# Value products of a half group: one block in every fourth unit instead of a piece in each

## What is computed

```python
q = _rms_norm(q, g_q)
k = _rms_norm(k, g_k)
logits = jnp.einsum('bhqd,bhkd->bhqk', q, k) * d ** (-0.5)
attn = jax.nn.softmax(logits, axis=-1)
o = jnp.einsum('bhqk,bhkd->bhqd', attn, v)
o = jnp.swapaxes(o, 1, 2).reshape(b, n, dim)
return o + o @ W_out
```

## Time and profile before

| | us |
|---|---|
| median of 3 runs | 2251.61 (2249.65 to 2253.29) |
| the profiled execution's own time | 2247.79 |
| its span | 2246.0 |
| attention loops, from the turn of unit 4 to the end of the tail, four batches together | 241.03 |
| PE busy, whole span | 2129.1 (95%) |
| VectorE busy | 1630.1 (73%) |
| ScalarE busy | 1293.8 (58%) |
| POOL busy | 527.2 (23%) |
| value products (L2023), mean duration of a pass in the first loop | 0.391 |
| turns (L2005), same | 0.274 |
| scores (L1989), same | 0.384 |

### The profile page before, as it was taken

The page is one execution under the profiler, slowest core; times in us unless marked ns, Lnnn a source line. Parts: engine busy times, 40 slices in busy tenths (PEclk is TensorE's granted clock), DMA queues, the critical chain, the costliest instruction groups (busy, mean ns, idle before and its releaser), DMA issues.

```text
span 2246.0 us, 135671 instructions
## 1 busy us (share of the span) xinstructions
PE 2129.1 (95%) x57232; PEld 1830.8 (82%) x57232; DVE 1630.1 (73%) x6269; ACT 1293.8 (58%) x5763; POOL 527.2 (23%) x2255
## 2 busy tenths in 40 slices
PE   5768999999989999999999999999999999999998
PEld 3654555645545899999999999999999999999997
DVE  7987967878678487777677776667766666766665
ACT  6765947758568345555556655555555545555553
POOL 2002121021120222332233322222222222222221
PEclk8559999999999999999999999999999999999999
DMA  5000000010010000000000000000000000000000
GB/s 208 3 2 1 1 1 1 1 57 1 1 57 1 22 5 5 5 1 1 1 1 1 1 11 1 1 11 1 1 11 1 1 1 10 1 1 11 13 9 14
DMA packets 8410, 26.49 MB, mean 12 GB/s; under 512 B 1028, under 2 KB 1352, under 8 KB 7880
## 3 DMA queue, kind: packets, MB, share of 16 engines
q1 hardware_dynamic: 7712, 23.07, 2.8%
q10 hardware_dynamic: 424, 0.07, 0.0%
HBM read 18.94 MB, written 4.19 MB: 10 GB/s over the span
## 4 chain that ended last, share of the span: by engine, by line
PE 80%; DVE 12%; ACT 4%; issue 2%; DMA 1%; POOL 0%; SPq 0%; DVEq 0%; POOLq 0%; ACTq 0%
PE psum L2257 54%; PE psum L2218 8%; PE psum L2005 3%; PE psum L1926 3%; PE psum L1968 2%; PE psum L2023 2%; PE psum L2103 2%; PE psum L1989 2%; DVE region_cols L1232 2%; DVE region_cols L1248 2%; DVE top L1425 2%; ACT region_rows L786 1%; PE psum L1945 1%; DMA region_cols<-in_L_cond_W_emb_dram 1%; PE psum L1902 1%
## 5 line engine op out<-in xcount | busy, mean ns | idle before, releaser
L2257 PE MATMUL psum<-partsA,region_w_hh 128*128 128x40 f16 x24576 | 855.3, 179 | 10.4 <-issue 4.8
L2257 PE MATMUL psum<-partsB,region_w_hh 128*128 128x40 f16 x24576 | 853.3, 179 | 0.6 <-issue 0.5
L2257 PEld LDWEIGHTS psum<-partsA,region_w_hh 128*128 128x128 f16 x24576 | 758.7, 96 | 37.1 <-issue 11.2
L2257 PEld LDWEIGHTS psum<-partsB,region_w_hh 128*128 128x128 f16 x24576 | 724.1, 96 | 1.1 <-issue 0.5
L599 POOL TENSOR_TENSOR region_w_b<-region_w_b 128x16 f32<-128x16 f32 x1022 | 245.3, 240 | 1078.4 <-DVE region_w_b L1751 1078.4
L1725 DVE TENSOR_REDUCE psum<-psum 128x8 f32<-128x32 f32 x1024 | 201.7, 197 | 198.6 <-PE psum L2257 187.7
L1061 ACT ACTIVATE mixA<-psum 128x8 f32<-128x8 f32 x512 | 95.3, 186 | 428.3 <-DVE psum L1725 428.3
L1075 ACT ACTIVATE region_w_b<-psum 128x8 f32<-128x8 f32 x1024 | 190.0, 186 | 144.0 <-DVE psum L1740 86.9
L601 POOL COPY region_work<-region_w_b 128x8 f32<-128x8 f32 x1024 | 230.9, 225 | 2.2 <-DVE region_w_b L1751 2.2
L1751 DVE TENSOR_TENSOR_SCAN region_w_b<-giveB,region_w_b 128x40 f32<-128x40 f32 x512 | 123.8, 242 | 129.0 <-ACT region_w_b L1075 129.0
L1732 DVE TENSOR_REDUCE psum<-psum 128x8 f32<-128x32 f32 x1024 | 191.1, 187 | 0.7 <-PE psum L2257 0.6
(11 more groups left out here) (265 smaller groups left out, 2820.9 us busy)
## 6 DMA issues: line engine op xcount, KB each, us to landing
region_rows<-in_x_dram SPq DMA_DIRECT2D x4, 1024.0 KB, 11.1
region_w_a<-in_L_cond_W_qkv_dram SPq DMA_DIRECT2D x1, 3072.0 KB, 23.4
region_w_hh<-in_L_cond_W_hh_dram SPq DMA_DIRECT2D x4, 768.0 KB, 6.3
region_w_a<-in_L_cond_W_ih_dram SPq DMA_DIRECT2D x1, 3072.0 KB, 9.9
out_dram<-region_w_b SPq DMA_DIRECT2D x12, 256.0 KB, 2.2
region_cols<-in_L_cond_W_emb_dram SPq DMA_DIRECT2D x1, 2048.0 KB, 19.5
region_cond<-in_cond_dram SPq DMA_DIRECT2D x1, 1024.0 KB, 11.0
region_w_a<-in_L_cond_W_out_dram SPq DMA_DIRECT2D x1, 1024.0 KB, 21.5
```

The costliest lines, as they stand in the source:

```text
L2257: made = e.matmul(k.slots(bank)[:, :, ch, :, 0:2], k.w16[:, 2 * read + c, part, NC * "rzn".index(g) + 2 * half + ch], k.parts[read][:, c]. ...
```

## The change

```diff
+VALUES_TURNS = {2: 0}
...
         if n + AHEAD < len(UNITS):
             pe_scores(e, k, b, n + AHEAD)
         pe_turn(e, k, b, n)
-        if n >= 4:
-            group, kt = divmod(n - 4, 4)
-            pe_weighted_values(e, k, b, group // 2, group % 2, kt)
+        if n >= 4 and n % 4 in VALUES_TURNS:
+            group, first = n // 4 - 1, VALUES_TURNS[n % 4]
+            for kt in range(first, first + NT // len(VALUES_TURNS)):
+                pe_weighted_values(e, k, b, group // 2, group % 2, kt)
             if group % 2 == 1 and kt == NT - 1:
                 pe_divide(e, k, b, group // 2)
```

## The result

| | before | after |
|---|---|---|
| median, us | 2251.41 (2249.65 to 2253.29, 4 runs) | 2285.44 (2284.99 to 2287.71, 4 runs) |
| profiled execution, its span | 2247.79, 2246.0 | 2287.71, 2286.0 |
| ratio, 95% interval | | 1.0152 (1.0137 to 1.0167) |

The changed kernel is 34.0 us slower by the medians. The forecast was 2287 against a median of 2251.6, 35.6 us more.

The account below looks back on a forecast made before the run. PE was taken as the bound at 1.98 us a unit, only 0.15 ahead of ScalarE. Half groups of 9.08 and 10.32 plus ends made 69.13 a batch, 35.6 more over four: 2287 us, range 2270 to 2300.

Parts of the forecast that it names:

- The ready work at the block's start: At the block's start in the attention loop, VectorE has only its copy left, 0.68; ScalarE one copy and exponentials, 0.60 + 1.34.
- PE's total decides: Rival for the attention loops: the block is absorbed, a half group costs 7.51, time 2240; chance 6%.
- The block's price: A block of 16 value products on PE takes 1.87 us; upper end 2.28 if standing together gains nothing.
- The two sums: Block start to next block start in the loop: 9.08 us for an undivided half group, 10.32 with a divide.
- The ends: Loop ends: turn 4 to the first block 5.25 us; seventh block (unit 30) to the tail block 3.81.
- The total: Turn 4 to the tail's end takes 69.13 us a batch, 8.90 more than before; four batches make 35.6.
- no change: Rival for the attention loops: stall and saving meet, a half group stays at 7.92, time near 2252; chance 4%.
- A short stall: Rival: the block's unit costs 3.28, the next three 1.83 each; half group 8.77, time 2275; chance 15%.
- The clock rival: PE's pauses in each unit lower the granted clock; at 0.65 the loops cost 115 us more, 2367; chance 3%.
- granted clock 1.00: Sign expected in the profile after: the granted clock stays at 1.00.
- no wait of value products for the divide copy: Sign in the loops: ScalarE's divide copy lies two units ahead of its reader, so that wait goes.
- one chain that starts with them: Chain after each block: scores, maxima, copy, reciprocal, maxima, neg_top, exponentials, copy, turn, next block; 9.08 us undivided.

Follow-up runs that it names:

- the half maxima with pieces: The kernel before with VectorE's row maxima over 256 of the 512 keys, value products still a piece in each unit: 2236.74 us, ratio 0.9947.
- the unit at 262.90 above: A regular unit of the kernel before reordered to turn, next scores, then the piece of value products, from unit 4 on: 2247.07 us, ratio 0.9991.

## Why the prediction was right

**What bounds the kernel.** Right: PE's full row of 1.98 a unit is a bound of its own, as the half maxima with pieces showed, and the others stand little behind it: in the undivided half group after the change turns that ScalarE's copy releases are still 1.83 apart (263.87 to 265.70).

**The ready work at the block's start.** The prediction gave VectorE only its copy, 0.68, because its maxima of unit m+2 "began before the turn". Its own rows say otherwise: the turn starts at 238.58 and the maxima at 238.78, and they run past the value products' start at 239.55. After the change the maxima of 256.95 and the copy of 258.09 keep VectorE at work until 258.77, 1.03 behind the block's start. The sum does not use the 0.68. The rejection of "PE's total decides" does, and it holds with 1.03 too, since that is still under the 2.31 which that case needs.

**The block's price.** 1.87 was taken, with 2.28 as the other end. Every block in the trace of after lasts 1.93 in the timeline and 1.87 to the next start, as the tail in the earlier trace rows, apart from two on a lowered clock. The prediction's estimate of 1.47 rested on the speedup that the Trainium skill, TensorE: Matmul & The Clock Gate, Part 3, "Measured speedup vs the span model", states for three column tiles. The four column tiles of these fp32 products took 1.87, and the measurement decides.

**The two sums.** Undivided 9.08 against 8.96, divided 10.32 against 10.29. The difference of the first lies in two links: the reciprocal to the next maxima (0.24 taken, 0.16 in the trace) and those maxima to neg_top (1.31 taken, 1.24); turn to block gives 0.03 back (0.97 taken, 1.00).

**The ends.** Turn 4 to the first block 5.25 against 5.33, the seventh block to the tail 3.81 against 3.83 (296.23 to 300.06).

**The total.** 69.13 a batch was forecast and 68.75 measured in the first: 8.52 more than before, not 8.90. The last batch has 8.96; its half groups are longer, 9.20 and 10.40, and so were those of before there (16.95 for two), so that the same figure for it came out by a shift of both. The two middle ones have 9.70 and 9.81, of which 1.2 and 1.4 are the clock (two blocks and two turns at a lowered clock, by the distances around them). Without that the four make 34.4, close to the 34.0 of the medians. The mechanism was right and the size 1.6 us too large by the medians.

**The profiled execution** differs from that of before by 40.0 us of span, not 34. 37.0 lie in the loops. 3.0 lie between the third loop and the fourth, where the granted clock is 0.72 in a stretch and eight projections (L1969) take 5.64 us for 3.49 before; 1.0 lies in the first turns of the first batch, at a clock of 0.78; and 1.0 comes off behind the last loop. That run is the slowest of the four, the others taking 2284.99 to 2285.79. The trace of before has such stretches too, at other places (0.80 and 0.91 in windows of 12 us between the third loop and the fourth), so they are not laid to the change, and the forecast's 35.6 is rightly held against the medians.

**The rivals.** PE's total (2240) and no change (2252) are out by the time itself. A short stall (2275) is out by the half groups' 8.96. The clock rival was half seen: it did fall for a few us in two loops and cost 2.6 us there, nothing like 115. The sign "granted clock 1.00" failed in those two, which say 0.98. And "no wait of value products for the divide copy" holds: there is none in the loop.

**What the prediction had narrower than it is.** It said that VectorE and ScalarE both wait for the scores behind the block, and it summed one chain that starts with them. For this order of PE's work that chain is the one in the trace, link by link, so the number is not luck. But ScalarE waited for the turn (0.67 and, behind a divide, 1.40), and with the scores ahead of the block 31.0 of 34.0 us stay. The chain through the turn is nearly as long, and the prediction did not price it; the cure that its account suggests gives back only 3 us.

## What to carry to other kernels

Where one engine feeds two others through short queues, what it does for later (here the value products, which nobody needs soon) is best cut to pieces that fit in the others' work and spread over all units. That is shown for this kernel alone: putting four pieces together saved PE 0.41 us a half group and made it 1.04 to 1.50 longer all the same, since a block of 1.87 outlasts the ready work of the others (in the undivided half group VectorE had 1.03 of it and then stood idle for 1.49). Taking the scores out from behind the block moved the wait to the turns, so a block is to be judged by everything that PE feeds. Before gathering work of one kind on the busiest engine, read at its place how many us of ready work each of its readers still has, and lay out one period by starts, not by busy time. Which engines set a pace can be told by making one cheaper in both kernels: cheaper maxima moved the kernel with blocks by 20.5 us and the one with pieces by 11.9, none of it in the latter's regular units. To price the order itself, compare the two kernels with the same edit (24.7 here), not one with the edit and one without.

## What was not expected of the hardware

The granted clock fell for some us inside two of the loops after the change. PE's windows of 4 us around the place in the second batch (us, PE busy, clock):

```profile
441.00:445.00 4.00, 3.02 (x20) 1.00 0.00 0
445.00:449.00 4.00, 3.35 (x20) 0.74 0.00 0
449.00:453.00 4.00, 3.46 (x40) 0.84 0.00 0
453.00:457.00 4.00, 3.66 (x48) 1.00 0.02 4
```

Before it fell PE was busy for 3.02 of 4 us, with idle times of up to 0.68 between its turns. In the two windows with 0.74 and 0.84 the lower of the two levels (1.2 GHz against 2.4) held for a part. The block at 448.77 lasted 2.66 us in the timeline, where all others of that loop last 1.93. In the trace of before no loop has it: the windows of all four, the first of them in the earlier trace rows, say 1.00. In the trace of after it stands at the turn and block of unit 30 in the second and third loop, but not in the first, where PE has the same starts and the same idle times up to there, nor in the fourth; what decides is open and was not tried.

The order of PE's kinds of work in a unit has a price of its own: turn, scores, value products takes 2.03 us where scores, turn, value products takes 1.98, with the same instructions (the unit at 262.90 above; its neighbours are the same within 0.01).
